# Softmax spreads ahead of the key turn, a fourth key copy on ScalarE, and stores one period later

## What is computed

```
x  = x + clip(modulated(x,  w0, style0) + b0, -256, 256)     # layer L0
kx = modulated(x, wk, stylek) + bk                            # layer K, 16 heads of 32 dims
A  = softmax(kx . kx / sqrt(32)) over the 16 heads of one token
y  = A . kx                                                   # 512 features again
x  = x + modulated(y, wo, styleo) + bo                        # layer O
```

## Time and profile before

| | |
|---|---|
| time, median of 3 runs | 765.31 us (760.2 to 765.8) |
| the profiled execution | 764.73 us, span of its instructions 762.9 us |
| TensorE, matmuls | 693.0 us busy, 91% of the span |
| VectorE | 626.1 us, 82% |
| ScalarE | 517.5 us, 68% |
| GpSimd | 151.7 us, 20% |
| DMA | 140.37 MB, mean 184 GB/s |
| TensorE's granted clock | 0.980 of full speed |

### The profile page before, as it was taken

One profiled execution on the slowest core, in us unless ns is written; L12 is line 12 of the kernel. 1 busy time (PEld: TensorE's weight loads), 2 busy tenths in 40 slices (PEclk: granted clock), 3 DMA queues, 4 the chain that ended last, 5 costly groups with the idle time before them and its releaser, 6 DMA issues.

```text
span 762.9 us, 21634 instructions
## 1 busy us (share of the span) xinstructions
PE 693.0 (91%) x8886; PEld 675.9 (89%) x8886; DVE 626.1 (82%) x1048; ACT 517.5 (68%) x1040; POOL 151.7 (20%) x139
## 2 busy tenths in 40 slices
PE   7999968999999999999999999999999899989896
PEld 6999968899888889988889998898999898889785
DVE  3689866998888898888899888889988888997662
ACT  4887855777667677666767766677767677765662
POOL 2024202222012222201222210222221122222200
PEclk9999999999999999999999999999999999989898
DMA  9267676467756676876567775657677665756853
GB/s 292 96 167 194 190 199 194 138 172 218 198 149 186 191 215 172 220 183 172 173 196 197 191 222 153 188 174 208 182 202 206 162 192 171 217 140 149 228 151 110
DMA packets 229666, 140.37 MB, mean 184 GB/s; under 512 B 141248, under 2 KB 223168, under 8 KB 229568
## 3 DMA queue, kind: packets, MB, share of 16 engines
q1 hardware_dynamic: 229568, 139.00, 65.0%
HBM read 71.85 MB, written 67.11 MB: 182 GB/s over the span
## 4 chain that ended last, share of the span: by engine, by line
DVE 53%; PE 22%; issue 9%; ACT 9%; DMA 4%; POOL 1%; SPq 1%; DVEq 0%; ACTq 0%; POOLq 0%
DVE p_bd L795 14%; PE y_ps L476 8%; PE lin_ps L413 7%; PE s_ps L458 6%; DVE o L773 5%; DVE x L754 5%; DVE v L744 4%; DVE x_lo L676 4%; DVE sc L759 3%; DVE x L752 3%; DVE sc L782 3%; DVE mx L764 3%; DVE p_turned L788 2%; DVE sc L766 2%; ACT sc L569 2%
## 5 line engine op out<-in xcount | busy, mean ns | idle before, releaser
L413 PE MATMUL lin_ps<-x_hi,w_hi 128*128 128x256 f32 x1008 | 287.3, 285 | 6.5 <-DVE w_lo L705 3.4
L413 PE MATMUL lin_ps<-x_lo,w_hi 128*128 128x256 f32 x1008 | 283.1, 281 | 0.0
L413 PE MATMUL lin_ps<-x_hi,w_lo 128*128 128x256 f32 x1008 | 282.9, 281 | 0.0
L383 POOL COPY k_bd<-k_rhs 32x1024 f32<-32x1024 f32 x128 | 147.4, 1151 | 568.1 <-DVE k_rhs L733 562.5
L413 PEld LDWEIGHTS lin_ps<-x_hi,w_hi 128*128 128x128 f32 x1008 | 191.3, 190 | 13.7 <-issue 13.5
L413 PEld LDWEIGHTS lin_ps<-x_lo,w_hi 128*128 128x128 f32 x1008 | 191.4, 190 | 0.2 <-issue 0.2
L413 PEld LDWEIGHTS lin_ps<-x_hi,w_lo 128*128 128x128 f32 x1008 | 191.3, 190 | 0.0
L413 PE MATMUL lin_ps<-y_hi,w_hi 128*128 128x256 f32 x528 | 150.4, 285 | 7.2 <-DVE y_lo L676 7.2
L413 PE MATMUL lin_ps<-y_lo,w_hi 128*128 128x256 f32 x528 | 149.3, 283 | 0.0
L413 PE MATMUL lin_ps<-y_hi,w_lo 128*128 128x256 f32 x528 | 149.2, 283 | 0.0
L509 ACT ACTIVATE x_hi<-x,style 128x256 fp32r<-128x256 f32 x252 | 113.0, 501 | 45.7 <-DVE x L754 39.4
(11 more groups left out here) (60 smaller groups left out, 727.1 us busy)
## 6 DMA issues: line engine op xcount, KB each, us to landing
x<-xT SPq DMA_DIRECT2D x32, 512.0 KB, 6.1
k_turned<-kx SPq DMA_DIRECT2D x32, 512.0 KB, 4.9
k_st<-k_turned SPq DMA_DIRECT2D x128, 128.0 KB, 3.1
v_turned<-k_rhs SPq DMA_DIRECT2D x32, 512.0 KB, 6.1
k_v<-v_turned SPq DMA_DIRECT2D x128, 128.0 KB, 3.2
y_turned<-y SPq DMA_DIRECT2D x128, 128.0 KB, 3.0
yr<-y_turned SPq DMA_DIRECT2D x32, 512.0 KB, 5.3
outT<-o SPq DMA_DIRECT2D x31, 512.0 KB, 4.0
```

The source lines that it names most:

```text
L383: pool.tensor_copy(k_bd[HD * r:HD * (r + 1), r], k_rhs[HD * r:HD * (r + 1)]).then_inc(g_kbd, 1)
L413: mm = pe.matmul(lin_ps[:, n % NLB, 0:T], w[:, k, m * P:(m + 1) * P], r[:, k, :], start=(q == 0), stop=(q == len(passes) - 1))
```

## The change

VectorE's period: `spread_probabilities(c2)` stands in front of `turn_k(c1)` instead of behind it, `turn_v(c2)` follows `turn_k` directly, both halves of `finish(c4)` come later, behind the low parts of the next x. GpSimd copies three of the four key groups (`POOL_GROUPS = 3`); the fourth is a ScalarE activation, `copy_keys`, behind the last `spread_some`, and `scores` waits for both. SP's period has the values back in front of `y` out, and the store of chunk i - 5 (finished one period before) between `y` out and `y` in; no store stands at the period's end.

```diff
--- before.py
+++ after.py
@@ -58,6 +58,7 @@
     GAIN = (float(SD) ** -0.5, 1.0, 1.0)
     SCALE = float(HD) ** -0.5
     WARM_STYLES, WARM_L0 = 9, 10
+    POOL_GROUPS = 3
     L0, K, O = range(3)
     assert HR == R == CT == 4 and TG == 8 and NG == 32 and TB == 2 * CT * QS
 
@@ -140,7 +141,7 @@
         y_out_landed, y_in_landed = sem("y_out_landed"), sem("y_in_landed")
         st_o = [sem(f"st_o{i}") for i in range(2)]
         g_eps, g_pad, g_warm, g_zero = sem("g_eps"), sem("g_pad"), sem("g_warm"), sem("g_zero")
-        g_kbd = sem("g_kbd")
+        g_kbd, a_kbd = sem("g_kbd"), sem("a_kbd")
         v_odd = sem("v_odd")
         pe_style, v_stt, v_style = sem("pe_style"), sem("v_stt"), sem("v_style")
         v_ssq, a_wsq = sem("v_ssq"), sem("a_wsq")
@@ -323,20 +324,20 @@
             y_to_dram(2)
             y_from_dram(2)
             v_to_dram(4)
-            store(1, 0, 1)
             for i in range(FIRST_LOOP, last - 1):
                 k_to_dram(i - 1)
                 k_from_dram(i - 1)
+                v_from_dram(i - 2)
                 y_to_dram(i - 3)
-                v_from_dram(i - 2)
+                store(i - 5, 0, 1)
                 y_from_dram(i - 3)
                 load_x(i + 2)
                 v_to_dram(i - 1)
-                store(i - 4, 0, 1)
             k_to_dram(last - 2)
             k_from_dram(last - 2)
+            v_from_dram(last - 3)
             y_to_dram(last - 4)
-            v_from_dram(last - 3)
+            store(last - 6, 0, 1)
             y_from_dram(last - 4)
             v_to_dram(last - 2)
             k_to_dram(last - 1)
@@ -379,7 +380,7 @@
             def spread_k(c):
 
                 pool.wait_ge(v_krhs, c + 1)
-                for r in range(R):
+                for r in range(POOL_GROUPS):
                     pool.tensor_copy(k_bd[HD * r:HD * (r + 1), r], k_rhs[HD * r:HD * (r + 1)]).then_inc(g_kbd, 1)
 
             pool.wait_ge(g_zero, 1)
@@ -448,7 +449,8 @@
 
             def scores(c):
 
-                pe.wait_ge(g_kbd, R * (c + 1))
+                pe.wait_ge(g_kbd, POOL_GROUPS * (c + 1))
+                pe.wait_ge(a_kbd, (R - POOL_GROUPS) * (c + 1))
                 if c:
                     pe.wait_ge(v_sc, c)
                 for x in range(2):
@@ -588,6 +590,13 @@
                 act.activation(p_bd[:, :, TG // 2 + t, :], p_turned[:], ACT.Copy,
                                scale=tok_mask[:, TG // 2 + t:TG // 2 + t + 1]).then_inc(a_pbd, 1)
 
+            def copy_keys(c):
+                if c == 0:
+                    act.wait_ge(g_zero, 1)
+                act.wait_ge(v_krhs, c + 1)
+                for r in range(POOL_GROUPS, R):
+                    act.activation(k_bd[HD * r:HD * (r + 1), r], k_rhs[HD * r:HD * (r + 1)], ACT.Copy).then_inc(a_kbd, 1)
+
             def l0_out(c, m):
                 if m == 0 and c >= NX1:
                     act.wait_ge(v_out, 2 * (c - NX1 + 1))
@@ -610,9 +619,9 @@
                     (c2, even_scores), (c0, l0_out, 0), (c2, exponentials), (c0, l0_out, 1), (c0, l0_out, 2),
                     (c0, x1_hi_of, 0), (c0, l0_out, 3), (c4, o_out, 0), (c0, x1_hi_of, 1), (c2, spread_some, 0),
                     (c4, o_out, 1), (c2, spread_some, 1), (i + 1, x_hi_of, 0), (c4, o_out, 2), (c2, spread_some, 2),
-                    (i + 1, x_hi_of, 1), (c4, o_out, 3), (c2, spread_some, 3), (c0, k_out, 0), (c3, y_hi_of, 0),
-                    (c0, k_out, 1), (c3, y_hi_of, 1), (c0, k_out, 2), (c0, k_out, 3), (c2, evacuate_y, 0),
-                    (c2, evacuate_y, 1)]
+                    (i + 1, x_hi_of, 1), (c4, o_out, 3), (c2, spread_some, 3), (c1, copy_keys), (c0, k_out, 0),
+                    (c3, y_hi_of, 0), (c0, k_out, 1), (c3, y_hi_of, 1), (c0, k_out, 2), (c0, k_out, 3),
+                    (c2, evacuate_y, 0), (c2, evacuate_y, 1)]
 
             act_head = [
                 (0, l0_out, 0), (0, l0_out, 1), (K, weights_hi, 0), (0, l0_out, 2), (0, x1_hi_of, 0), (0, l0_out, 3),
...
@@ -800,8 +810,8 @@
                 c0, c1, c2, c3, c4 = range(i, i - 5, -1)
                 return [
                     (c2, merge_scores), (c2, subtract_maxima), (c0, make_x1, 0), (c2, normalise), (c0, make_x1, 1),
-                    (c0, x1_lo_of, 0), (c0, x1_lo_of, 1), (c1, turn_k), (c2, spread_probabilities), (c4, finish, 0),
-                    (c2, turn_v), (c4, finish, 1), (i + 1, x_lo_of, 0), (i + 1, x_lo_of, 1), (c3, y_lo_of, 0),
+                    (c0, x1_lo_of, 0), (c0, x1_lo_of, 1), (c2, spread_probabilities), (c1, turn_k), (c2, turn_v),
+                    (i + 1, x_lo_of, 0), (i + 1, x_lo_of, 1), (c4, finish, 0), (c4, finish, 1), (c3, y_lo_of, 0),
                     (c3, y_lo_of, 1)]
 
             dve_head = [
@@ -823,12 +833,12 @@
                 (2, y_lo_of, 0), (2, y_lo_of, 1)]
             dve_tail = [
                 (last - 3, merge_scores), (last - 3, subtract_maxima), (last - 1, make_x1, 0), (last - 3, normalise),
-                (last - 1, make_x1, 1), (last - 1, x1_lo_of, 0), (last - 2, turn_k), (last - 1, x1_lo_of, 1),
-                (last - 3, spread_probabilities), (last - 3, turn_v), (last - 5, finish, 0), (last, x_lo_of, 0),
-                (last, x_lo_of, 1), (last - 4, y_lo_of, 0), (last - 4, y_lo_of, 1), (last, make_x1, 0),
-                (last, make_x1, 1), (last, x1_lo_of, 0), (last, x1_lo_of, 1), (last - 2, merge_scores),
-                (last - 2, subtract_maxima), (last - 1, turn_k), (last - 2, normalise), (last - 2, turn_v),
-                (last - 2, spread_probabilities), (last - 5, finish, 1), (last - 1, merge_scores),
+                (last - 1, make_x1, 1), (last - 1, x1_lo_of, 0), (last - 1, x1_lo_of, 1),
+                (last - 3, spread_probabilities), (last - 2, turn_k), (last - 3, turn_v), (last, x_lo_of, 0),
+                (last, x_lo_of, 1), (last - 5, finish, 0), (last - 4, y_lo_of, 0), (last - 4, y_lo_of, 1),
+                (last, make_x1, 0), (last, make_x1, 1), (last, x1_lo_of, 0), (last, x1_lo_of, 1),
+                (last - 2, merge_scores), (last - 2, subtract_maxima), (last - 1, turn_k), (last - 2, normalise),
+                (last - 2, turn_v), (last - 2, spread_probabilities), (last - 5, finish, 1), (last - 1, merge_scores),
                 (last - 1, subtract_maxima), (last - 3, y_lo_of, 0), (last - 3, y_lo_of, 1), (last, turn_k),
                 (last - 1, turn_v), (last - 1, normalise), (last - 1, spread_probabilities), (last - 4, finish, 0),
                 (last - 4, finish, 1), (last, merge_scores), (last, subtract_maxima), (last, normalise),
```

More of the change, by code:

```diff
@@ L633, in _ @@
                 (0, y_hi_of, 0), (0, y_hi_of, 1), (1, evacuate_y, 0), (1, evacuate_y, 1), (2, even_scores),
[L634 to L641, removed]
+                (0, o_out, 0), (2, exponentials), (0, o_out, 1), (0, o_out, 2), (0, o_out, 3), (3, copy_keys),
+                (6, x_hi_of, 0), (6, x_hi_of, 1), (4, k_out, 0), (2, spread_some, 0), (2, spread_some, 1),
+                (2, spread_some, 2), (2, spread_some, 3), (4, k_out, 1), (4, k_out, 2), (4, k_out, 3),
+                (5, x1_hi_of, 0), (5, x1_hi_of, 1), (2, evacuate_y, 0), (2, evacuate_y, 1), (3, even_scores),
+                (1, y_hi_of, 0), (1, y_hi_of, 1), (1, o_out, 0), (3, exponentials), (1, o_out, 1), (1, o_out, 2),
+                (1, o_out, 3), (5, k_out, 0), (4, copy_keys), (3, spread_some, 0), (3, spread_some, 1),
+                (3, spread_some, 2), (3, spread_some, 3), (5, k_out, 1), (5, k_out, 2), (5, k_out, 3),
+                (3, evacuate_y, 0), (3, evacuate_y, 1), (2, y_hi_of, 0), (2, y_hi_of, 1)]
             act_tail = [
@@ L646, in _ @@
                 (last - 3, spread_some, 2), (last - 3, spread_some, 3), (last, x_hi_of, 0), (last, x_hi_of, 1),
-                (last - 1, k_out, 0), (last - 4, y_hi_of, 0), (last - 1, k_out, 1), (last - 4, y_hi_of, 1),
-                (last - 1, k_out, 2), (last - 1, k_out, 3), (last, l0_out, 0), (last, l0_out, 1), (last, l0_out, 2),
-                (last, x1_hi_of, 0), (last, l0_out, 3), (last, x1_hi_of, 1), (last - 3, evacuate_y, 0),
-                (last - 3, evacuate_y, 1), (last - 2, even_scores), (last, k_out, 0), (last - 2, exponentials),
@@ L651, in _ @@
-                (last, k_out, 1), (last, k_out, 2), (last, k_out, 3), (last - 5, o_out, 2), (last - 5, o_out, 3),
-                (last - 3, y_hi_of, 0), (last - 3, y_hi_of, 1), (last - 2, spread_some, 0),
-                (last - 2, spread_some, 1), (last - 2, spread_some, 2), (last - 2, spread_some, 3),
-                (last - 1, even_scores), (last - 4, o_out, 0), (last - 4, o_out, 1), (last - 1, exponentials),
-                (last - 2, evacuate_y, 0), (last - 2, evacuate_y, 1), (last - 4, o_out, 2), (last - 4, o_out, 3),
@@ L661, in _ @@
-                (last - 2, o_out, 1), (last, evacuate_y, 0), (last, evacuate_y, 1), (last - 1, y_hi_of, 0),
-                (last - 1, y_hi_of, 1), (last - 2, o_out, 2), (last - 2, o_out, 3), (last - 1, o_out, 0),
```

(13 more changed lines are left out.)

27 lines of the change are left out of this document (15 added, 12 removed).

## The result

The changed kernel took 725.24 us (median of 4, 724.39 to 731.09), the kernel before beside it 764.4 us (median of 4). The ratio is 0.9513, 95% interval 0.945 to 0.9576: faster by 4.9%. The forecast was 732 us, range 720 to 758.

What follows compares the result with a forecast made beforehand. TensorE, idle 1.64 us a period waiting for the value transposes, was taken to bound the kernel. 764.7 - 30.5 (24 periods from 22.37 to 21.1 us) - 2 (tail) = 732 us, range 720 to 758 us.

Steps and rivals of the forecast that it cites:

- The bound: TensorE's loop: it idles 1.64 us a period waiting for the value transposes, and the change removes that wait.
- The floor: TensorE's loop period without its wait for the transposes: 22.37 - 1.64 = 20.73 us.
- low parts 1.58 us more expected: VectorE's four low parts of x, now beside GpSimd's copies: 1.65 us alone, 1.58 us more there.
- The merge: VectorE's next merge of scores: cannot start before +21.42, low parts of y end at +20.82, leaving 0.6 us.
- The 2.4 us: VectorE's low parts held by two whole GpSimd copies under the port lock: merge 0.2 us late, 5 us in all.
- Slack used up exactly: ScalarE's period: with the 1.05 us copy, y is evacuated by +20.71, and even_scores is due at +20.73.
- The DMA ring: Loop transfers from ScalarE's y_hi through keys out, keys in and yr back to y_hi: about 20.4 us.
- longest: Upper length given for the DMA ring in the loop: 3.1 + 4.9 + 10.1 + 7.1 = 25.2 us.
- late landings: Loop: landings 1 us late in a third of the periods, 0.35 us each; period taken as 21.1 us.
- Head and tail: Outside the loop: tail counted as 2 us shorter (3.3 at most), head unchanged, give or take 1.
- Slower: Rival: the DMA ring, yr late behind the store, makes loop periods above 22.7 us; 783 us at 23.2. Chance 0.07.
- the second rival: Loop: DMA ring or ScalarE's copy takes most gain back; periods 21.5 to 22.2 us, 742 to 757 us. Chance 0.25.

Runs made afterwards that it cites:

- e6: Kernel before with one edit in VectorE's loop, the first half of finish moved behind the value transposes: 729.49 us, ratio 0.9558.
- e7: Kernel before with one edit in VectorE's loop, the spreads moved ahead of the key turn: 722.42 us, ratio 0.949.
- e3: Kernel before with only the fourth key copy moved from GpSimd to ScalarE, VectorE's and SP's orders unchanged: 738.9 us, ratio 0.9694.
- e8: Changed kernel with a second ScalarE copy each period, into a tile nobody reads: 743.26 us, ratio 0.9756.
- e9: e7 plus the ScalarE key copy for the first five chunks alone, GpSimd making four copies afterwards: 721.61 us, ratio 0.9446.
- e11: Changed kernel with one more 512 KB transfer to DRAM issued right ahead of yr each period: 754.07 us, ratio 0.9895.
- e1: Kernel before with only VectorE's new order (loop and tail), GpSimd making all four copies, SP as before: 732.66 us, ratio 0.9609.
- e4: Changed kernel without the ScalarE copy, so VectorE's and SP's new orders with four GpSimd copies: 723.55 us, ratio 0.9489.
- e5: Changed kernel without SP's new order, so VectorE's new order and the ScalarE copy: 723.76 us, ratio 0.9487.
- e12: e1 with the store at the period's end one period later (chunk i - 5 instead of i - 4): 721.92 us, ratio 0.9455.
- e10: Changed kernel with y out ahead of the values in, and the store behind yr instead of ahead: 721.0 us, ratio 0.9455.

## Why the prediction was right, step by step

**The bound.** TensorE's wait of 1.64 us for the transposes was the whole loss: e6 and e7 take the path to the transposes below the limit by two different edits and get 0.956 and 0.949. The contention with GpSimd, 3.24 us of that path, was its cause in this sense: e7, in which spreads (1.67 us) and first `finish` (0.69 us) are free of it, removes the wait, and e3, which takes 0.85 us of it away, removes just over half. But e6 shows that the order alone would also do. The floor was taken at 20.73 us; the best loops measured 20.76.

**VectorE.** Spreads 1.66 expected, 1.67 measured; transposes 2.3 us ahead expected, 2.0 measured; low parts 1.58 us more expected, 1.56 measured. The merge does not start late: 0.99 us of idle time stand before it. The 2.4 us that I worked out from the rule of the Trainium skill (SBUF — State Buffer, SBUF: two separate sides) would have been too much; the measured 1.56 decides. The single rows show why:

```profile
L686 DVE SCALAR_TENSOR_TENSOR x_lo<-x,style,x_hi x4: 452/864/1268, 372.6 to 375.4; 128x256 fp32r<-128x256 f32 x4
```

The four took 0.45, 1.27, 1.25 and 0.47 us. So two of them were held, each by one whole copy, as the rule says. But a held one costs 0.8 us more than a free one, not 1.2, since its own 0.47 us lie within the 1.26 us of a held one: one low part got through with each copy.

**ScalarE.** The copy at 1.05 us, as taken. "Slack used up exactly" is nearly so: it runs without a wait at 20.67 us a period (20.62 by e8). In each of the eight periods in which it waited for `yr`, the time from one `even_scores` to the next was 20.8 us and that wait (0.90 us: 21.69; 0.33 us: 21.11).

**The DMA ring.** 3.1 + 3.3 + 9.2 + 4.8 = 20.4 was expected; the changed kernel's rows give 3.1 + 2.9 + 9.6 + 4.6 = 20.2. Choosing keys out near its least was right; the ring's "longest", 25.2 us, was not, since it has keys out at its median of 4.9 us: with the largest, 7.3, it is 27.6. **The term that was mis-sized is the 0.35 us a period for late landings**: ScalarE waited for `yr` 8 times, a third of the periods as taken, but 3.7 us in all, 0.46 us each instead of 1. And the waits mostly did not reach TensorE, whose score matmuls follow each other at 20.73 to 20.87 us but for the three periods with a gap and two others (21.07 and 21.11). The period is 20.93 instead of 21.1, which is 24 x 0.17 = 4.1 us. Most of what the loop lies above e9's are TensorE's three gaps (2.9 of 3.8 us), not landings: the prediction had no term for them, and that its 0.35 us came as near as it did is in part luck.

**Head and tail.** Tail 3.5 us instead of 2, head 1.6 instead of 0, give or take 1. That the head would gain was not foreseen. The six runs with the copy on ScalarE throughout reach the loop at 127.6 to 128.2 us and the seven without it at 128.6 to 130.5, but e9, with the copy in the head alone, at 129.4: that the copy is the cause is not shown. The largest wait there is shorter as expected, 3.7 to 2.3 us:

```profile
PE s_ps L460 <- POOL k_bd L384: 2.3, 1, 2.3
```

The sum: 35.2 + 3.5 + 1.6 = 40.3 us, against 30.5 + 2. The loop's 4.7 us over the forecast are the 4.1 above and 24 x 0.026: the period before was 22.40 us in the mean, not 22.37.

**The rivals.** "Slower" had the right mechanism with too little transfer in it (e11). What none of my cases held is that two of the three parts were not needed: e7, a single swap, reaches 722.42 us, and the copy and SP's order only matter where VectorE's new order has pushed `finish` late (e1, 732.66 us) and each of them alone mends that (e4, e5). A smaller slip: the second rival's period of 21.5 us and more was priced at 757 us at its top, but 22.2 us gives 764.7 - 24 x 0.17 - 2 = 758.6 us.

## What to carry to other kernels

Ask how much the wait is worth before asking what causes it: 1.64 us had to go, the change brought the transposes forward by 3.8 us against the mark (18.29 to 14.52), and two single edits that took 1.5 us or more (e6, e7) gave most or all of the gain. Where GpSimd and VectorE meet, put behind the instruction that starts GpSimd what is either immune (here the transposes, 1.29 us beside it as without it) or not waited for. And when a step is moved back, look for the queue whose next entry waits for it: a store that waits for `finish` and goes out right ahead of keys out cost 24 x 0.39 us (e1 against e12).

## What the runs showed of the hardware that was not expected

- The first VectorE instruction behind the one that releases GpSimd escapes the contention, since it starts 0.14 to 0.16 us before GpSimd's first copy: `finish` 0.69 us in that place, 1.40 us behind the transposes (e7), 1.52 us behind four spreads. GpSimd pays a part: its first copy beside that `finish` takes 1.44 us, against 1.23 beside a spread, and its four copies 5.15 us instead of 4.78.
- From then on the two engines take turns, one VectorE instruction to one copy. Four spreads took 4.02 us beside four GpSimd copies and 4.02 us beside three (e3, median of the loop). Only the `finish` behind them gained from the missing copy, 1.52 to 0.67 us. The rows of the four spreads of the earlier trace rows (shortest, median, longest, in ns) show it: one is free, three are held by a copy each, and the fourth copy is left for `finish`.

```profile
L795 DVE TENSOR_SCALAR p_bd<-p_turned,tok_mask x4: 484/1258/1261, 386.9 to 389.6; 128x512 f32<-128x512 f32 x4
```

- A VectorE instruction that waits for GpSimd is shown as busy, not as idle. VectorE's busy time fell from 626.1 to 582.7 us with the same list of instructions.
- TensorE stood idle for 0.5 to 2.2 us at three places of its list, as far as can be told because its instructions came late. The profile puts that down to "issue"; the packets of the instruction queue tell when to suspect it (e10).
